# Local attention's feed-forward stored in eleven blocks, its outer residual added on GpSimd, and expert outputs scattered by token

## The reference

```python
h = h @ w1 + b1                       # 256 -> 2 x 682
a, g = jnp.split(h, 2, axis=-1)
h = a * jax.nn.gelu(g, approximate=False)
x = x + h @ w2 + b2                   # 682 -> 256
...
x = _layernorm(x + _L2_ffn_ref(x, ...), axis=-1)
```

```python
logits = xt @ Wg.T
topk_logits, topk_idx = jax.lax.top_k(logits, TOP_K)
w = jax.nn.softmax(topk_logits, axis=-1)
h = jax.nn.gelu(jnp.einsum('th,ehi->tei', xt, W1) + b1, approximate=False)
o = jnp.einsum('tei,eih->teh', h, W2) + b2
y = jnp.einsum('te,teh->th', gates, o)
```

## Time and profile before

| | |
|---|---|
| median of three runs | 3248.57 us (3239.93 to 3249.87) |
| profiled execution: its time / its span | 3245.3 us / 3243.3 us |
| mean granted clock of PE | 0.928 of 2.4 GHz |
| PE busy | 2813.8 us (87%) |
| VectorE busy | 1858.8 us (57%) |
| ScalarE busy | 1582.8 us (49%) |
| GpSimd busy | 678.3 us (21%) |
| bytes moved by DMA | 80.63 MB |

### The profile page before, as it was taken

One profiled execution on the slowest core, in us unless ns is written; L12 is line 12 of the kernel. 1 busy time (PEld: TensorE's weight loads), 2 busy tenths in 40 slices (PEclk: granted clock), 3 DMA queues, 4 the chain that ended last, 5 costly groups with the idle time before them and its releaser, 6 DMA issues. The chain is left out here.

```text
span 3243.3 us, 53378 instructions
## 1 busy us (share of the span) xinstructions
PE 2813.8 (87%) x18513; PEld 1724.1 (53%) x18545; DVE 1858.8 (57%) x4564; ACT 1582.8 (49%) x4328; POOL 678.3 (21%) x758
## 2 busy tenths in 40 slices
PE   8678988679999997779888999999998889969993
PEld 4635652435555554346556553455533355659992
DVE  5655765548788775858566642266423547843334
ACT  6325953237777774841346532155421539813330
POOL 3110030112212210112035620065300003311113
PEclk9878999789999999889999999999999989969996
DMA  1010020200000001000010010000000000241112
GB/s 72 2 19 1 2 86 0 72 1 2 2 2 2 1 13 52 1 14 2 17 41 1 1 64 0 7 1 1 4 26 14 7 23 2 80 174 36 36 33 83
DMA packets 36129, 80.63 MB, mean 25 GB/s; under 512 B 9089, under 2 KB 24530, under 8 KB 32050
## 3 DMA queue, kind: packets, MB, share of 16 engines
q1 hardware_dynamic: 30962, 64.68, 5.6%
q0 software_dynamic: 4368, 11.93, 1.3%
q10 hardware_dynamic: 560, 0.93, 0.1%
HBM read 63.18 MB, written 14.02 MB: 24 GB/s over the span
## 5 line engine op out<-in xcount | busy, mean ns | idle before, releaser
L2553 ACT ACTIVATE scores<-scores,min 128x128 f32<-128x128 f32 (+7 forms) x256 | 198.5, 775 | 87.0 <-DVE min L2536 82.8
L2534 DVE TENSOR_SCALAR zero_marks<-psum 128x128 f32<-128x128 f32 (+7 forms) x256 | 192.2, 751 | 67.3 <-PE psum L2466 65.5
L2536 DVE CUSTOM_DVE_ANT_0 scores<-psum,zero_marks 128x128 f32<-128x128 f32 (+7 forms) x256 | 194.1, 758 | 30.4 <-issue 1.6
L2473 PE MATMUL psum<-ident,scores 128*128 128x128 f32 x1152 | 172.9, 277 | 16.7 <-ACT probsT L2570 13.8
L2570 ACT ACTIVATE probsT<-psum 128x128 f32<-128x128 f32 (+7 forms) x256 | 163.0, 637 | 31.7 <-PE psum L2473 31.1
L3996 PE MATMUL psum<-Hn,W 128*128 128x512 f32 x384 | 169.7, 605 | 8.0 <-PEq L54 8.0
L1701 ACT ACTIVATE XT<-psum,early_weights 128x128 f32<-128x128 f32 x312 | 89.0, 368 | 175.3 <-PE psum L1621 175.3
L2473 PEld LDWEIGHTS psum<-ident,scores 128*128 128x128 f32 x1152 | 123.3, 141 | 55.9 <-issue 30.6
L1621 PE MATMUL psum<-early_weights,XT 128*128 128x128 f32 x1248 | 149.3, 278 | 1.5 <-DVE XT L1666 1.5
L1621 PEld LDWEIGHTS psum<-early_weights,XT 128*128 128x128 f32 x1248 | 144.5, 193 | 8.2 <-issue 5.4
L3844 POOL TENSOR_TENSOR probs<-probs,stat 128x512 f32<-128x512 f32 (+1 forms) x128 | 123.2, 986 | 101.0 <-DVE stat L3808 98.6
(11 more groups left out here) (635 smaller groups left out, 6704.1 us busy)
## 6 DMA issues: line engine op xcount, KB each, us to landing
W<-in_L3f_W SPq DMA_DIRECT2D x16, 1024.0 KB, 12.8
L3f_y_rows<-early_weights SPq DMA_DIRECT2D x39, 128.0 KB
early_weights<-in_L2f_Wqkv SPq DMA_DIRECT2D x2, 1536.0 KB
W<-in_L2f_W SPq DMA_DIRECT2D x2, 1536.0 KB
XT<-in_xT SPq DMA_DIRECT2D x1, 2048.0 KB, 7.6
Xtok<-in_xtok SPq DMA_DIRECT2D x1, 2048.0 KB
L0f_rows<-Xtok SPq DMA_DIRECT2D x4, 512.0 KB, 2.9
W<-in_L0f_W SPq DMA_DIRECT2D x2, 1024.0 KB
```

The costliest lines, as they stand in the source:

```text
L2473: ins = pe.transpose(turned[:, kt * P:(kt + 1) * P], Sc[:, i % ROT, kt * P:(kt + 1) * P], K.ident[:])
L2534: dve.tensor_scalar(zero[:, i % 2, 0:n], sc(i)[:, 0:n], 0.0, -NEG, ALU.is_equal, ALU.mult)
L2536: dve.tensor_tensor_reduce(Sc[:, i % ROT, 0:n], sc(i)[:, 0:n], zero[:, i % 2, 0:n], 1.0, -NEG, ALU.add, ALU.min, low[:, i % ROT:i % ROT + ...
L2553: act.activation(p, p, ACT.Exp, bias=low[:, i % ROT:i % ROT + 1], scale=-1.0, accum_out=sums[:, u % 2, h:h + 1]).then_inc(s["exp_done"], 1)
```

## The change

It has three parts.

1. *Feed-forward of local attention.* 682 is 5 x 128 + 42. The five whole blocks of value and gate stay; the two remainders of 42, each padded to 64, share one block, value on partitions 0 to 63 and gate on 64 to 127. So the last four steps (m = 5) have two matmuls for four; ScalarE's gelu reads the upper half of the bank and writes the lower half of its buffer, and VectorE writes the product twice, to partitions 0 to 63 and to 64 to 127 of `GT`. The last 64 rows of `W2` are stored twice likewise. `add_residual` (first layer) ends each token block with one 64-row matmul for each feature block, the one on the lower partitions and the other on the upper; `finish_features` (second layer) takes 64 rows for the last matmul of each sum.
2. *Outer residual.* The phase "step" is gone. GpSimd adds x0 to x1, both halves, during the gated stage of the second layer.
3. *Expert outputs.* Routing computes for each slot a row `row_at`: block 1 + 16 * choice + token tile, and the token's place in it; unused slots get row 0. `token_at` is derived from it. GpSimd scatters each tile of outputs to `y_rows` by `row_at`, in turn with the gathers, and counts `y_free` up when the scatter before has landed; VectorE's copy waits for `y_free`. In the last phase SP loads the first choices and ScalarE the second ones with four plain transfers each, 512 rows of 1 KB in one.

```diff
@@ -291,7 +291,8 @@
...
-                    last = pe.matmul(K.bank[h][:], wt(k, h, j), src(k, j), start=(k == 0), stop=(k == n_k - 1))
+                    own = slice(0, P if k < n_k - 1 else HALF)
+                    last = pe.matmul(K.bank[h][:], wt(k, h, j)[own, :], src(k, j)[own, :], start=(k == 0), stop=(k == n_k - 1))
@@ -1287,7 +1288,7 @@
...
-    y_rows = nc.dram_tensor("L3f_y_rows", [SLOT_TILES * P, D], F32, kind="Internal").ap()
+    y_rows = nc.dram_tensor("L3f_y_rows", [(2 * NT + 1) * P, D], F32, kind="Internal").ap()
@@ -1321,13 +1322,7 @@
...
-            @block.gpsimd
-            def _(pool):
-                for k, tiles in enumerate(groups):
-                    for t in tiles:
-                        for i in range(2):
-                            pool.indirect_dma_start(out=Y[:, t, i, :], out_offset=None, in_=y_rows[:, :],
-                                                    in_offset=bass.IndirectOffsetOnAxis(ap=slot[:, i, t:t + 1], axis=0)).then_inc(gathered[k], 16)
+            chosen_rows = lambda i, k: y_rows[(i * NT + k * GT + 1) * P:(i * NT + (k + 1) * GT + 1) * P].rearrange("(t p) d -> p t d", p=P)
@@ -1361,7 +1356,7 @@
...
                     dve.wait_ge(s["bias_out"], (k + 1) * GT)
-                    dve.wait_ge(gathered[k], 16 * 2 * GT)
+                    dve.wait_ge(gathered[k], 16 * 2)
                     for i in range(2):
@@ -1380,6 +1375,8 @@
...
                 for k in range(len(groups)):
+                    act.dma_start(Y[:, k * GT:(k + 1) * GT, 1, :], chosen_rows(1, k)).then_inc(gathered[k], 16)
+                for k in range(len(groups)):
                     act.wait_ge(s["turned"], k + 1)
@@ -1391,20 +1388,22 @@
...
                 for k in range(len(groups)):
+                    sp.dma_start(Y[:, k * GT:(k + 1) * GT, 0, :], chosen_rows(0, k)).then_inc(gathered[k], 16)
+                for k in range(len(groups)):
                     sp.wait_ge(s["normed"], k + 1)
...
@@ -1529,7 +1529,6 @@
...
                 dve.drain()
-                dve.tensor_copy(slot[:], sl[:, 0])
@@ -1555,11 +1554,14 @@
...
                 step(dve.tensor_copy, found[:, 0:2], K.bank[7][:, 0:2 * SLOT_TILES].rearrange("p (a g) -> p a g", a=2))
-                step(dve.scalar_tensor_tensor, found[:, 0], found[:, 0], float(P), found[:, 1], ALU.mult, ALU.add)
-                dve.tensor_copy(token_at[:], found[:, 0])
-
-
-def run_experts(nc, K, x_rows, y_rows, W1, W2, b1, weights_in, token_at, w_at):
+                dve.scalar_tensor_tensor(row_at[:], found[:, 0], float(P), found[:, 1], ALU.mult, ALU.add)
+                step(dve.tensor_scalar, found[:, 2], found[:, 0], NT + 0.5, float(NT), ALU.is_gt, ALU.mult)
+                step(dve.tensor_tensor, found[:, 0], found[:, 0], found[:, 2], ALU.subtract)
+                step(dve.tensor_scalar, found[:, 0], found[:, 0], 1.0, 0.0, ALU.subtract, ALU.max)
+                dve.scalar_tensor_tensor(token_at[:], found[:, 0], float(P), found[:, 1], ALU.mult, ALU.add)
+
+
+def run_experts(nc, K, x_rows, y_rows, W1, W2, b1, weights_in, token_at, row_at, w_at):
@@ -1574,29 +1576,39 @@
...
             def _(pool):
-                for g in range(SLOT_TILES):
+                def gather(g):
                     if g >= 3:
...
+                def scatter(g):
+                    pool.wait_ge(s["y_out"], g + 4)
+                    pool.indirect_dma_start(out=y_rows[:, :], out_offset=bass.IndirectOffsetOnAxis(ap=row_at[:, g:g + 1], axis=0),
+                                            in_=Yt[:, g % 3, :], in_offset=None).then_inc(stored[g % 3], 16)
+
+                pool.sem_inc(s["y_free"], 3)
+                for g in range(3):
+                    gather(g)
+                for g in range(SLOT_TILES):
+                    if g + 3 < SLOT_TILES:
+                        gather(g + 3)
+                    if g >= 1:
+                        pool.wait_ge(stored[(g - 1) % 3], 16 * ((g - 1) // 3 + 1))
+                        pool.sem_inc(s["y_free"], 1)
+                    scatter(g)
+
             @block.sync
...
                 for q in range(3):
-                    sp.sem_inc(stored[q], 16)
-                with sp.Fori(0, TURNS) as i:
-                    for q in range(3):
-                        sp.wait_ge(s["y_out"], i * 3 + q + 4)
-                        sp.dma_start(y_rows[bass.ds(i * (3 * P) + q * P, P), :], Yt[:, q, :]).then_inc(stored[q], 16)
-                for q in range(3):
-                    sp.wait_ge(stored[q], 16 * (TURNS + 1))
+                    sp.wait_ge(stored[q], 16 * TURNS)
@@ -1671,7 +1683,7 @@
...
                     dve.wait_ge(s["down_done"], i * 3 + q + 4)
-                    dve.wait_ge(stored[q], i * 16 + 16)
+                    dve.wait_ge(s["y_free"], i * 3 + q + 1)
                     dve.tensor_copy(Yt[:, q], K.bank[6][:, 0:D]).then_inc(s["y_out"], 1)
@@ -3588,12 +3604,20 @@
...
     for l in range(L2D):
-        two = lambda a, axis: np.concatenate([pad(a[..., :L2HID], axis, HIDP), pad(a[..., L2HID:], axis, HIDP)], axis=axis)
+        def two(a):
+            left, right = a[..., :L2HID], a[..., L2HID:]
+            own, other = (pad(v[..., WHOLE * P:], a.ndim - 1, HALF) for v in (left, right))
+            return np.concatenate([left[..., :WHOLE * P], right[..., :WHOLE * P], own, other], axis=-1)
+
+        def down(a):
+            whole = rows(a[:WHOLE * P])
+            rest = np.concatenate([pad(a[WHOLE * P:], 0, HALF)] * 2)
+            return np.concatenate([whole, rest[:, None, :]], axis=1)
...
@@ -3891,10 +3915,16 @@
...
                 pe.wait_ge(K.late, weights_at)
+            whole = n_k - 1 if split else n_k
             for n, (h, j) in enumerate(steps):
-                for k in range(n_k):
+                for k in range(whole):
                     ins = pe.matmul(K.bank[n][:], wt(k, h), src(k, j), start=(k == 0), stop=(k == n_k - 1))
-                ins.then_inc(s["done"], 1)
+                if not split:
+                    ins.then_inc(s["done"], 1)
+                elif h == DC - 1:
+                    for i in range(DC):
+                        own = slice(i * HALF, (i + 1) * HALF)
+                        pe.matmul(K.bank[n - h + i][:], wt(whole, i)[own, :], src(whole, j)[own, :], start=False, stop=True).then_inc(s["done"], 1)
@@ -3991,11 +4021,18 @@
...
                                     pe.wait_ge(s["out"], n - 3)
-                                for part in range(2):
+                                for part in range(2 if m < WHOLE else 1):
                                     for k in range(DC):
-                                        ins = pe.matmul(K.bank[2 * (n % 4) + part][:], W1[:, k, (part * HC + m) * P:(part * HC + m + 1) * P],
+                                        at = part * WHOLE + m if m < WHOLE else 2 * WHOLE
+                                        ins = pe.matmul(K.bank[2 * (n % 4) + part][:], W1[:, k, at * P:(at + 1) * P],
                                                         Hn[:, k, j * BLK:(j + 1) * BLK], start=(k == 0), stop=(k == DC - 1))
                                 ins.then_inc(s["done"], 1)
+
+                        @block.gpsimd
+                        def _(pool):
+                            if l == L2D - 1:
+                                for k in range(DC):
+                                    pool.tensor_tensor(x1[:, k, :], x1[:, k, :], x0[:, k, :], ALU.add)
@@ -4004,26 +4041,27 @@
...
                                     act.wait_ge(s["out"], n - 1)
-                                act.activation(ge[:, n % 2, :], K.bank[2 * (n % 4) + 1][:], ACT.Gelu, bias=b1[:, HC + m:HC + m + 1]).then_inc(s["gelu_done"], 1)
+                                if m < WHOLE:
+                                    act.activation(ge[:, n % 2, :], K.bank[2 * (n % 4) + 1][:], ACT.Gelu, bias=b1[:, WHOLE + m:WHOLE + m + 1]).then_inc(s["gelu_done"], 1)
+                                else:
+                                    act.activation(ge[0:HALF, n % 2, :], K.bank[2 * (n % 4)][HALF:, :], ACT.Gelu, bias=b1[HALF:, 2 * WHOLE:]).then_inc(s["gelu_done"], 1)
...
                                 dve.wait_ge(s["gelu_done"], n + 1)
-                                dve.scalar_tensor_tensor(out=GT[:, m, j * BLK:(j + 1) * BLK], in0=K.bank[2 * (n % 4)][:], scalar=b1[:, m:m + 1],
-                                                         in1=ge[:, n % 2, :], op0=ALU.add, op1=ALU.mult).then_inc(s["out"], 1)
+                                if m < WHOLE:
+                                    dve.scalar_tensor_tensor(out=GT[:, m, j * BLK:(j + 1) * BLK], in0=K.bank[2 * (n % 4)][:], scalar=b1[:, m:m + 1],
+                                                             in1=ge[:, n % 2, :], op0=ALU.add, op1=ALU.mult).then_inc(s["out"], 1)
+                                else:
+                                    for rows_of in (slice(0, HALF), slice(HALF, P)):
```

(13 more changed lines are left out.)

39 lines of the change are left out of this document (22 added, 17 removed).

## The result

The changed kernel takes **3217.91 us** (median of 4 runs, 3215.92 to 3221.36) beside 3248.88 for the kernel before (4 runs): a ratio of 0.991, with a 95% interval of 0.9898 to 0.9922. That is 31 us less where 40.6 were forecast against the median (3248.57 to 3208), or 37.3 against the profiled execution. The profiled execution after has a span of 3214.1 us and a time of its own of 3215.92, 29.4 under the 3245.3 of before.

The account below looks back on a forecast made before the run. Bounds: PE passes, one phase holding PE up, and the gathers at the end. Terms sum to 37.3 us, taken from the profiled 3245.3 to give 3208 us; range 3197 to 3221, the forecast's own 3202 to 3214.

Parts of the forecast that it names:

- Eleven blocks: Gated feed-forward, both layers: 6.9 us less PE work, 0.75 more behind it, 6.1 gained per layer, 12.3 us in all.
- Half-height pair, first layer: First layer's down product: 64-row matmuls overlap in pairs, less one more VectorE addition behind PE; 1.5 us gained.
- Remainder, second layer: Second layer's finishing product: 64-row matmuls save nothing and change height eight times; 2.0 us lost.
- The outer residual: Phase between second layer's gated and finishing products: its additions move to GpSimd under the gated stage; 6.9 us gained.
- PE's clock: Behind the 2.6 us gaps of both layers: clock drop counted as lost in one of two, net 0.
- Routing and expert loop: Routing: three more small VectorE operations, one cast less, 0.6 us lost; expert loop: GpSimd's scatters fit the slack, 0.
- Rival 4: Expert loop: the scatter chain paces the experts, kernel slower than before, 3265 us at a landing of 8.5; chance 0.03.
- The last scatter: Between last output copy and last phase: scatter landing and waking take 3.0 us where 2.4 passed; 0.6 us lost.
- The last phase: End of the kernel: plain loads replace 32 gathers, VectorE sets the pace, 63.7 us become 43.9; 19.8 us gained.
- rivals 2 and 3: Loads pace the last phase, 3226 us, halfway 3217, chance 0.12; changing heights costs more than it gives, 3215, chance 0.10.
- rival 5: More gain than forecast: ScalarE's issues short, both gaps at full clock, no height price in layer two; 3201 us, chance 0.11.

Follow-up runs that it names:

- kernel 8: The changed kernel with the remainder of the down product at full height in both layers, no 64-row matmuls: 3208.06 us, ratio 0.9922.
- kernel 7: The kernel before with the outer residual alone changed (additions on GpSimd, step phase gone, twelve blocks kept): 3228.45 us, ratio 0.9988.
- Kernels 1 and 6: The changed kernel with expert loop and last phase in one block, 3213.06 us; the changed kernel with one more GpSimd drain three tiles earlier, 3211.01 us.
- kernel 2: The changed kernel without the scatter of the last tile: 3217.99 us, ratio 0.9911.

## Why the prediction was right, and where it was not

**Eleven blocks** (12.3): right. The gated products take 6.9 us less in layer one (77.47 for 84.33) and 7.0 in layer two, the gap behind them 0.75 more.

**Half-height pair, first layer** (+1.5): right. 2.04 us less on PE (kernel 8) less 0.65, by which the next stage's first product stands further behind (4.68 us idle for 4.03): 1.4. The pair takes 1.06 us to the next full product, as in the earlier trace rows; my 0.1 more for its entry was not needed there.

**Remainder, second layer** (-2.0): right, 2.2 to 2.3.

**The outer residual** (+6.9): right to the tenth, 6.93 in kernel 7; GpSimd beside the gated products costs nothing.

**PE's clock** (0): a fair bet, and here good luck. Behind the gap of 2.58 us the profiled execution kept the full clock in both layers, 1.8 us more than I counted. Of the ten profiled kernels that have this gap in the first layer the clock had fallen in three, of the nine that have it in the second, in eight, at 1.4 to 1.6 us each. Behind 1.83 us it fell in none.

**Routing and expert loop** (-0.6, 0): right; 0.7 us from the start of the routing to the last y copy, tiles at the same distance. Rival 4 is dead: data of the last scatter, whose 128 rows all go to one row, landed 2.06 us behind its issue, the semaphores of all 39 scatters were full 3.13 to 3.14 us behind theirs, and GpSimd passes its wait at 3.2 us. The Trainium skill (DMA: Bandwidth & Descriptors, Anatomy of one DMA) warns of surprisingly long write receipts in HBM; no scatter of this trace shows one, with some 1.1 us between the last one's data and its semaphore.

**The last scatter** (-0.6): **this is the step that failed**. "A scatter at the gathers' 2.8 and 0.2 for waking makes 3.0" counted the landing alone. SP passed its wait at 3167.18, 3.4 us behind the copy, close to that. But a block ends when every engine has ended, and GpSimd, whose drain was over 31 us earlier in the kernel before, now ended last: its drain lasts 6.4 us behind the last of 78 indirect transfers. The term is -5.5, 4.9 worse. The same trace held the warning: 4.5 us behind the last of 39 gathers, hidden. I did not ask what a block's end costs the engine to which the work was moved. Kernels 1 and 6 show the cause by taking the wait or the length away.

**The last phase** (+19.8): right mechanism, a little more, 21.3. ScalarE's issues take 2.52 us (3.4), the first bias addition comes 4.4 us in (5.7), VectorE never waits for a load; groups last 8.1, 8.1, 7.3 and 7.4.

In sum the changed places gave 35.3 us for 37.3: -4.9 at the junction, +1.5 for the last phase, +1.8 for the clock, small change elsewhere. The other 6 us up to 29.2 are unchanged code, later in this execution. The outcome lies in the range, near rivals 2 and 3 in time, but by neither's mechanism, and 4 us above the forecast's own range of 3202 to 3214. That the wide range held is partly luck: it was opened for ScalarE's issues, the heights and the clock, none of which cost what it allowed, and what filled it was a drain that no term had, together with unchanged code. Three of its figures were also off by themselves: the high end's terms give 3208 + 8.5 + 3.3 = 3219.8, not 3221, rival 5's terms (1.9, 1.8 and 2.0) give 3202.3, not 3201, and with both gaps at the low clock the clock's term would be -1.8, where the bound says -4. None of them changes the outcome.

## What to carry to other kernels

When work moves to an engine, ask what that engine's end of phase costs and whether it is now the last to end; drain GpSimd early, where it idles, or let no one wait for its end, if many indirect transfers stand behind it. An earlier start of an engine is no gain by itself: copies that come behind DMA issues, or products that run at the lower clock, gave 3 us back. Cost small edits stage by stage; unchanged code moves by several us between executions.

## What the runs showed of the hardware

GpSimd's drain goes on for 2.4 us behind the last of 4 or 16 indirect transfers, 3.1 to 4.2 behind 32, 4.2 to 4.5 behind 39, 6.1 behind 74 and 6.4 behind 77 or 78, in kernel 2 with all of them landed, while behind plain additions it ends within 0.07. A scatter of 128 rows of 1 KB costs 0.98 us of issue, about as much as a gather, and lands 3.14 us behind its start in the changed kernel (2.41 to 3.16 in kernel 8, on the other chip). A matmul of 512 columns that takes 64 rows between full-height ones costs 0.28 us extra. The same kernel, the one before, took 3246 to 3247 us on one chip and 3233.8 on another.
